# Cross attention, shared net and routed experts on one core: attention and the shared net become one block of engine programs

## The reference

```
x = x + Wo(attention(layernorm(x) Wq, ctx Wk, ctx Wv, masks)) + bo      # 16 heads, 64 keys
z = layernorm(x)
e = argmax(z @ gate_w.T)                                                # one of 2 experts
shared = relu(z @ sw1 + sb1) @ sw2 + sb2                                # 512 -> 2048 -> 512
routed = sum over experts i of relu((z if e == i else 0) @ w1[i] + b1[i]) @ w2[i] + b2[i]
x = x + routed + shared
```

## Time and profile before

| | |
|---|---|
| three runs | 1908.34, 1908.87, 1910.06 us (median 1908.87) |
| profiled execution | 1907.19 us, its span 1905.5 us, granted TensorE clock 0.986 of full |
| PE | 1826.0 us busy, 96% |
| ACT | 820.3 us busy, 43% |
| DVE | 798.1 us busy, 42% |
| POOL | 509.2 us busy, 27% |
| DMA | 214.44 MB, mean 113 GB/s |

### The profile page before, as it was taken

How to read it: one execution, slowest core, us unless ns; L and a number is a source line. 1 busy time by engine, 2 the same in 40 slices (tenths; PEclk the granted TensorE clock), 3 DMA queues, 4 the chain that set the end, 5 groups by cost and what they waited for, 6 DMA issues and landing times.

```text
span 1905.5 us, 33426 instructions
## 1 busy us (share of the span) xinstructions
PE 1826.0 (96%) x11516; PEld 1149.4 (60%) x11517; DVE 798.1 (42%) x1649; ACT 820.3 (43%) x1441; POOL 509.2 (27%) x477
## 2 busy tenths in 40 slices
PE   8979999999799999999999998999999999999997
PEld 6335444544466666666666665666666666666664
DVE  6967778777244433342333333222222222222222
ACT  3645555554333334334444443333333333433333
POOL 2047777776101111221100001122221112122111
PEclk9989999999899999999999999899999999999998
DMA  9235555555942333223344493822121111212100
GB/s 322 83 86 147 161 166 166 175 157 150 267 110 78 100 95 94 90 86 121 121 121 136 151 302 114 247 56 56 51 62 45 38 44 47 60 44 61 51 24 15
DMA packets 230151, 214.44 MB, mean 113 GB/s; under 512 B 130864, under 2 KB 172336, under 8 KB 229680
## 3 DMA queue, kind: packets, MB, share of 16 engines
q1 hardware_dynamic: 221120, 188.09, 34.2%
q0 software_dynamic: 8944, 25.19, 4.3%
HBM read 129.57 MB, written 59.02 MB: 99 GB/s over the span
## 4 chain that ended last, share of the span: by engine, by line
PE 67%; DMA 1%; DVE 1%; issue 1%; ACT 1%; SPq 1%; POOL 0%; POOLq 0%; ACTq 0%
PE pH L998 34%; PE pY L1010 33%; DMA e_split<-s_el 1%; DVE s_el L1341 1%; ACT room_a L1023 0%; ACT s_eh L1255 0%; DVE room_a L1029 0%; SPq L1146 0%; ACT room_a L1021 0%; DMA room_a<-rows_room 0%; SPq L1147 0%; POOL rows_room L1409 0%; DVE room_a L1037 0%; DVE s_work L1296 0%; SPq L980 0%
## 5 line engine op out<-in xcount | busy, mean ns | idle before, releaser
L998 PE MATMUL pH<-room_a,room_w 128*128 128x256 f16 (+1 forms) x6336 | 770.8, 272 | 29.4 <-DMA room_a<-rows_room 10.3
L1010 PE MATMUL pY<-room_w,room_a 128*128 128x512 f16 (+1 forms) x3120 | 755.2, 380 | 6.1 <-DVE room_a L1029 6.1
L998 PEld LDWEIGHTS pH<-room_a,room_w 128*128 (+1 forms) x6336 | 613.1, 98 | 215.6 <-issue 33.3
L1029 DVE TENSOR_TENSOR room_a<-room_a 128x256 f16<-128x256 f32 (+1 forms) x528 | 237.6, 450 | 900.9 <-ACT room_a L1023 900.8
L1010 PEld LDWEIGHTS pY<-room_w,room_a 128*128 128x128 f16 x3120 | 304.7, 98 | 270.0 <-DVE room_a L1029 7.1
L1021 ACT ACTIVATE room_a<-pH,e_bsel,sc 128x256 f32<-128x256 f32 (+1 forms) x272 | 151.7, 558 | 432.9 <-PE pH L998 408.1
L1021 ACT ACTIVATE room_a<-pH,b1s,sc 128x256 f32<-128x256 f32 x256 | 144.1, 563 | 360.1 <-PE pH L998 360.1
L1205 POOL TENSOR_TENSOR room_a<-room_a,s_brow 128x512 f32<-128x512 f32 x32 | 42.4, 1344 | 543.6 <-DVE room_a L1037 543.6
L470 PE MATMUL pO<-room_w,room_b 128*128 (+1 forms) x768 | 172.7, 382 | 4.8 <-DVE room_b L682 4.8
L1023 ACT ACTIVATE room_a<-pH,e_bsel,sc 128x256 f16<-128x256 f32 (+1 forms) x272 | 149.5, 550 | 0.0
L1023 ACT ACTIVATE room_a<-pH,b1s,sc 128x256 f16<-128x256 f32 x256 | 142.4, 556 | 0.0
(11 more groups left out here) (175 smaller groups left out, 1341.7 us busy)
## 6 DMA issues: line engine op xcount, KB each, us to landing
s_er<-in_w SPq DMA_DIRECT2D x64, 512.0 KB, 5.0
room_w<-e_split SPq DMA_DIRECT2D x8, 2048.0 KB, 18.6
rows_room<-in_x SPq DMA_DIRECT2D x32, 256.0 KB, 3.0
room_a<-in_sw SPq DMA_DIRECT2D x32, 256.0 KB, 4.2
room_b<-in_x SPq DMA_DIRECT2D x32, 256.0 KB, 3.7
s_split<-room_a SPq DMA_DIRECT2D x64, 128.0 KB, 3.8
x_scratch<-room_b SPq DMA_DIRECT2D x32, 256.0 KB, 4.0
z_split<-room_b SPq DMA_DIRECT2D x32, 256.0 KB, 4.1
```

The lines of the kernel that those rows point to most:

```text
L998: mm = q.matmul(self.pH[j % 2][:, 0:rows], w[:, k, j * P:(j + 1) * P], zt[:, u, k, 0:rows], start=(n == 0), stop=(n == 3 * KC - 1))
L1010: mm = q.matmul(self.pY[u][r][:, :], h[:, j % self.HR, r * P:(r + 1) * P], w[:, j, :], start=(j == 0 and n == 0), stop=(j == HC - 1 and n ...
L1029: q.tensor_tensor(self.hl[:, j % self.HR, 0:rows], self.hf[:, j % self.HR, 0:rows], self.hh[:, j % self.HR, 0:rows], ALU.subtract).then_in ...
```

## The change

1. Blocks 1 and 2 are one block: each engine runs its attention program and then its shared-net program, with no meeting point between. The buffers of the shared net (`er`, `eh`, `el`, `cacc`, `brow` and others) lie on attention's `room_b`, `pH` is the two halves of attention's `pS[1]`, and `pY` is `pP`, `pG` and `pO`.
2. The last row block's residual, second norm and gate leave the attention loop: DVE does them behind `lo_h` of the chunks 1 to 4 of shared tile 0, ACT behind `relu` of chunk 4, SP stores the block's x1 and z behind `load_e(0)`. The bias row's load comes after all x1 and z stores have landed.
3. Row blocks 0 and 1 are both normed in the setup (`early`), `lo_x` of both on DVE.
4. `AT = (8, 13)`. The sort is in three parts at chunks 4, 7 and 10 of tile 1.
5. `by_tiles` stands at chunk 12 of tile 14; the first gathered rows are transposed ahead of the last store of expert weights. The result, bias and store of shared tile 15 move into the experts' block: DVE's part behind `lo_h` of chunk 1, POOL's at the head, SP's ahead of expert 1's weights.

```diff
 setup, ACT
-    if n == NF - 5:
-        normal(act, 0, 0)
+    if n in (NM + 20, NM + 23):
+        normal(act, 0, (n - NM - 20) // 3)
 setup, DVE (i = n - NM)
-    if i == 15:
-        stats(dve, 0, 0); stats_done(dve, 0, 0); aggregate(dve, 0, 0); add_eps(dve, 0, 0); shifts(dve, 0, 0)
+    if i in (13, 16):
+        stats, stats_done, aggregate, add_eps (dve, 0, (i - 13) // 3)
+    if i in (15, 18):
+        shifts(dve, 0, (i - 15) // 3)
+    if i in (23, 26):
+        lo_x(dve, 0, (i - 23) // 3)
 DVE, last row block
+def last_block(part):
+    g, u = SUB // N - 1, N - 1
+    if part == 0: residual(dve, g, u)
+    if part == 1: stats2_done, aggregate2, add_eps2 (dve, g, u)
+    if part == 2: agg2_done, shifts2, gate (dve, g, u)
+    if part == 3: pick(dve, g, u)
 shared_net
-AT = (10, 13)
+AT = (8, 13)
 shared_net, SP
     for q in range(2, Q):
         load_quarter(...); load_quarter(...)
+    sp.wait_ge(attended, SUB)
     load_e(0)
-    sp.dma_start(brow[:, :], sb2.partition_broadcast(P)).then_inc(S["brow_in"], 16)
+    last_block()                       # store_x1 and store_z of row block 31
     for u in range(2):
         sp.wait_ge(stored["x1_out", u], 16 * SUB // 2)
         sp.wait_ge(stored["z_out", u], 16 * SUB // 2)
+    sp.dma_start(brow[:, :], sb2.partition_broadcast(P)).then_inc(S["brow_in"], 16)
     load_r(0)
...
-    store_e(2 * TILES - 1)
-    store(TILES - 1)
+    sp.wait_ge(S["h"], HC * (TILES - 1))
     enet.transpose_rows(sp, 0)
+    store_e(2 * TILES - 1)
 shared_net, ACT
     step(act, g, u, 0, net.relu, j, lambda u, j: b1s[:, j:j + 1])
+    if N * g + u == 0 and j == 4:
+        last_block()                   # normal2 of row block 31
 shared_net, DVE
     step(dve, g, u, 0, net.lo_h, j)
-    if j == 3:
+    if N * g + u == 0 and 0 < j < 5:
+        last_block(j - 1)
+    if j == 3 and not past(g, u):
         step(dve, g, u, -1, net.result, 16, 16)
-    if j == 3 and isinstance(g, int) and g == 0 and u == 1:
-        slots()
-    if j == 13 and last_tile(g, u):
+    if isinstance(g, int) and N * g + u == 1 and j in (4, 7, 10):
+        {4: row_ranks, 7: tile_experts, 10: row_slots}[j]()
+    if j == 12 and N * g + u == TILES - 2:
         by_tiles()
         pick_rows(dve, enet, iz, order, 0, 0, enet.S["pick_z"])
 experts, SP
     sp.dma_start(b2r ...)
+    store_rows(sp, snet, res_d, TILES - 1)
     sp.wait_ge(snet.S["e_out"], 64 * TILES)
 experts, POOL
+    add_bias(pool, TILES // N - 1, 1, snet, brow)
     for u in range(N):
         pool.wait_ge(snet.S["out", u], 16 * TILES // N)
 experts, DVE
     step(dve, g, u, 0, net.lo_h, j)
+    if j == 1 and first_tile(g, u, 0):
+        snet.result(dve, TILES // N - 1, 1, 16, 16)
```

More of the change, by code:

```diff
@@ new lines, in xattn_ffn @@
+                f = a
+                w_in = f.enter_context(nc.semaphore("e_w_in"))
+                for net in (snet, enet):
+                    net.pH = [pS[1][:, n * 512:(n + 1) * 512] for n in range(2)]
+                    net.pY = [[pP[:, 0:DM], pP[:, DM:2 * DM]], [pG[:, :], pO[:, :]]]
+                enet.S["pick_z"] = f.enter_context(nc.semaphore("e_pick_z"))
+                snet.S["e_out"] = f.enter_context(nc.semaphore("s_e_out"))
+                room = (f, take, er, sc, wA, wB, room_w, cacc, order, inv, is1, is0, eh, el, iz, brow, w_in, snet, enet, stored, first_in)
@@ L403, in store_z @@
[L403 to L421, removed]
-                                if isinstance(g, int) and g == SUB // N and u == 0:
-                                    load_w1_w2(1)
@@ L1039, in result, with add_bias, store_rows @@
         v.then_inc(self.S["o"], 1)
+def add_bias(q, g, u, net, brow):
+    q.wait_ge(net.S["o"], net.tile(g, u) + 1)
+    for r in range(net.R):
+        v = q.tensor_tensor(net.ob[:, u, r, :], net.ob[:, u, r, :], brow[:, :], ALU.add)
+    v.then_inc(net.S["ob"], 1)
+def store_rows(sp, net, res_d, t):
+    sp.wait_ge(net.S["ob"], t + 1)
+    sp.dma_start(net.rows(res_d, t), net.ob[:, t % net.N, :, :]).then_inc(net.S["out", t % net.N], 16)
 def weight_set(room):
@@ new lines, in shared_net, with sem @@
+    N, S, step = net.N, net.S, net.step
+    def sem(n):
+        S[n] = f.enter_context(nc.semaphore("s_" + n))
+    for n in ("brow_in", "e_am", "e_red", "e_step", "ranks", "sort", "inv0", "blank", "scattered", "inv_in", "ordered", "eh", "el", "cacc", "rb1", "seen"):
+        sem(n)
+    S.update(first_in)
+    for u in range(N):
+        sem(f"e_in{u}")
+    rb1 = take([2 * HC])
+    work = take([6, SUB])
+    worki = take([SUB], I32)
+    half_at = take([SLOT_SUBS])
+    half_sub = take([1])
@@ new lines, in shared_net, with first_tile, last_tile, past @@
+    late = take([TILES, 2])
+    seen = take([2, TILES])
+    pI = net.pZ
+    pR = pI[:, 1, 0:2 * SUB]
+    EXP_STEPS = 18
+    SORT_STEPS = 30
+    PASS = TILES // 2
+    AT = (8, 13)
+    def first_tile(g, u, d):
+        return isinstance(g, int) and N * g + u + d == 0
+    def last_tile(g, u):
+        return isinstance(g, int) and N * g + u == TILES - 1
+    def past(g, u):
+        return isinstance(g, int) and N * g + u == TILES
+    def rows(t, g, u):
+        return net.rows(t, N * g + u)
@@ new lines, in shared_scalar, with split_hi, body @@
+    def shared_scalar(act, last_block):
+        def split_hi(n, i):
+            act.wait_ge(S[f"e_in{n % 2}"], 16 * TILES + 32 * (n // 2 + 1))
+            at_least(act, S["e_out"], 64 * n)
+            act.activation(eh[:, i, :, :], er[:, n % 2, i, :, :], ACT.Copy, scale=sc[:, (EW1, EW2)[i]:(EW1, EW2)[i] + 1]).then_inc(S["eh"], 1)
+        def body(g):
+            for u in range(N):
+                for j in range(HC):
+                    step(act, g, u, 0, net.relu, j, lambda u, j: b1s[:, j:j + 1])
+                    if N * g + u == 0 and j == 4:
+                        last_block()
+                    for h, at in enumerate(AT):
+                        if j in (at, at + 2) and PASS <= N * g + u < TILES:
+                            if N * g + u == PASS and j == AT[0]:
+                                act.wait_ge(S["e_step"], EXP_STEPS)
+                            split_hi(2 * (N * g + u - PASS) + h, (j - at) // 2)
+        unrolled(TILES // N, body)
```

1497 lines of the change are left out of this document (752 added, 745 removed).

## The result

| | before | after |
|---|---|---|
| median | 1909.42 us (4 runs, 1908.34 to 1910.06) | 1881.27 us (4 runs, 1880.21 to 1883.23) |
| profiled execution, span | 1907.2, 1905.5 us | 1883.2, 1881.4 us |

The ratio after to before is 0.9854, with a 95% interval of 0.9837 to 0.9871: some 28 us faster. The spans differ by 24.1 us; the profiled execution of before lay about 2 us under its median, that of after 2 above.

The account below looks back on a forecast made before the run. PE was busy 1826.0 of 1905.5 us, so only its holes and slow stretches could be won. A 3.0 + B 0 + C 5.5 + D 12 + E1 6.6 + E2 -1.3 = 25.8 us off 1908.9: 1883, range 1870 to 1893.

Parts of the forecast that it names:

- A: Setup, two row blocks normed there: first mask 3.1 us earlier, taken as a gain of 3.0 us, bounds 1 to 4.
- B: No barrier after attention: 11.1 us won, lost again to a 9 us hole in shared tile 0; 0, bounds -4 to +11.
- C: Sort in three parts in shared tile 1: none reaches PE, gain 5.5 us, bounds 4 and 5.6.
- D: AT = (8, 13), shared tiles 8 to 15: ACT's store waits at chunk 13 go, gain 12 us, bounds 9 and 13.
- E1: Turn into the experts: hole of 4.3 us instead of 10.33, restart 2.3 instead of 2.9; gain 6.6, bounds 5 and 8.
- E2: Expert tile 1: its transposes land late behind expert 1's weights on SP; -1.3 us, bounds 0 and -5.
- every step keeps its distance: Attention after the first mask: later steps keep their spacing, so the setup's gain of 3.0 us carries on.
- Rival 1: Shared tile 0: second weight buffer lands before PE asks, barrier's gain of 11 us kept; 1872 us, chance 0.20.
- Rival 2: New holes in setup, shared net and expert tile 1 larger than counted: sum 13.5, 1895 us; chance 0.13.
- Rival 3: All 528 chunks: halves of one PSUM tensor slow matmul or eviction; 1938 us at 4% a chunk, chance 0.03.
- Rival 4: Shared net: the early chunk does nothing, PE keeps 9.5 us of waits; 1893 us, chance 0.04.

## Why the prediction was right

It said 1883, a gain of 25.8 us; 1881.27 was measured, a gain of 28.1 by the medians. Step by step, in us of the two profiled executions, whose spans differ by 24.1 only:

| step | predicted | measured | from |
|---|---|---|---|
| A | 3.0 | 3.2 | attention ends at 484.58, was 487.76 |
| B | 0 | -0.8 | to chunk 2 of tile 1 56.3, was 55.6 (539.41 + 1.5 chunks, less 487.76) |
| C | 5.5 | 5.5 | next six chunks 15.6, were 21.2 |
| D | 12 | 12.1 | PE ends the shared net at 1164.96; without a loss it would be 1163.5, from 556.52 |
| E1 | 6.6 | 6.2 | hole and restart 4.58 + 2.5, were 10.33 + 2.9 |
| E2 | -1.3 | -2.2 | expert tile 0 without its first 36 matmuls, hole at tile 1 included: 39.8 (46.18 - 6.38), was 37.6 (44.38 - 6.80); 2.04 of it the hole |
| sum | 25.8 | 24.0 | spans: 24.1 |

**A** was the term that was sized wrong, and that it agrees in the table is luck. I had added 1.9 us to the setup; the last split ended at 107.7, 0.2 later than before, as the two `lo_x` and the norms fitted between splits that wait for PE anyway. So the first mask came 5.2 us sooner and not 3.1. In the profiled execution 2.2 us of it were lost again: from the first mask to the last it took 347.2 us (113.63 to 460.80), before 344.9 (118.87 to 463.82), 1.2 of the difference behind POOL's hole, where the scores took 7.03 us and 5.82 at the same place of the trace before. But in the nine other traces with the new setup that stretch took 344.7 to 346.7 us: "every step keeps its distance" holds within 2 us, and the profiled execution is the one of ten in which attention ended last. Over all traces the setup gives 5.1 us (482.7 against 487.8), 2 more than the sum had. With that, and with B as the means have it (55.3 against 55.5, +0.2), the steps add up to 26.9, which covers some 3 of the 4 us between the 24.0 of the table and the 28.1 of the medians; the last one stays open.

**B** held in every part: the start without a hole; the load at 532.8 (I had 535.5, with attention's end at 487.76; with 484.58 that is 532.3); the wait of 13.6 us at chunk 13 (about 12); the hole of 9.2 (9; 7.0 to 9.7 in the five traces that have it, so the exact figure is partly luck). Rival 1 failed as a forecast, but its price was right: with the load in time the two runs gave 44.7 against 56.3, 11.6 us, where I had written 11. The row that decided was the wait of 0.19 us in the earlier trace rows: a load just in time means that an earlier start buys nothing, as long as the load doesn't come earlier too.

**C and D** held alone and together. D kept two waits of ACT where I had one at most (6.1 us in sum), both without weight for PE: 0.6 and 0.4 us of PE's waiting are left in tiles 8 to 15. VectorE's 4.43 us beside POOL's reduction stayed, as said; the split behind it started late but was not stretched itself (1.27 us at 902.08).

**E1** held in sum; half of it is the early pick of rows, which my working had not priced apart. Its hole is the same in every trace, but its restart is not: behind 4.5 to 4.6 us of idle the 36 matmuls took 5.5 to 7.0 us, so 1.6 to 3.1 were lost where I had 2.3. **E2** was sized 0.9 too small; the mechanism, transposes behind the 8 MB load on SP, is shown by the run that puts them first. Rival 2's sum has a slip: its terms give 14.1 and not 13.5, the time is 1895 either way. Rival 3 is out: `first` and `second` stay at 273 and 380 ns a matmul, and a chunk at 2.605 us. Rival 4 is out by the run with that edit alone.

## What to carry to other kernels

Before a barrier is taken away, look for the load that lands closest to its use behind it: with a wait near zero there, the barrier is its cover, and the two must go together. What a queue holds beside such a load counts by its pieces, not by its bytes, most of all what stands ahead of it: write a constant in whatever layout has the longest runs. Try an edit alone on the old kernel and hold it against its stretch in the new one: where the two agree, as for the early chunk (11.6 and 12.1 us) and the sort (5.1 and 5.5), the sum of terms can be trusted; where an edit gives nothing alone and much with another, as the barrier and the load, the two share a hole. And take more than one trace of the same code before a difference of 3 us between two traces is called a term.

## What the runs showed that I had not expected

- 16.5 KB in 4224 pieces took 18.1 to 23.9 us to land in twelve traces, in 128 pieces 5.6 us in two. They hold up the issuing too: on SP the load of 1 MB took 5.9 to 12.6 us to issue behind them in nine traces, 0.98 to 1.30 ahead of them in three, 0.95 behind the 128 pieces in two.
- A hole of 2.37 us ahead of the last two of attention's products costs nothing or 1.6 to 1.7 us: behind the first of the two holes 24 matmuls took 5.35 us in one trace and 6.94 in another of a kernel alike up to there, behind the second 7.04 or 6.96. In the changed kernel's trace the granted clock is 1.00 behind the first (469 to 475 us) and 0.50 behind the second (478 to 480 us). Such places are a part of the spread between profiled executions of the same code. The two rows are of the changed kernel and of the one with load and rows first:

```profile
469.11 5.35 PE L480 MATMUL pO<-room_w,room_b 128*128 128x512 f16 x24 [2.37 <-DVE room_b L692]
```

```profile
466.82 6.94 PE L480 MATMUL pO<-room_w,room_b 128*128 128x512 f16 x24 [2.38 <-DVE room_b L692]
```
